# Another sequence of calls on four engines of a fused metaformer layer, with the mixing rows' transposing behind that of t's rows

## What is computed

```
# mixer, on patches of 3x3 positions (j = 0..8), 96 channels
x_norm = sqrt(sum_c patch^2)                  # after a layer norm over channels
y      = patches . w_mask / (x_norm * w_norm) # 512 prototypes, 9 positions
best   = argmax over (prototype, position)
max_act = the patch's channels at the best position     # gathered row of x
vc_vec  = w_mask[best prototype]                        # gathered row
inp  = concat(max_act*max_sim + vc_vec*(1-max_sim), sims of that prototype)
h    = leaky_relu(inp @ w_i1.T + b);  vcs = tanh(h @ w_i2.T + b)
h2   = relu(vcs @ w_l1.T + b) @ w_l2.T + b;  x = x + conv1x1(h2)
# feed-forward, each position a row of 96, weights and inputs rounded to 8 bits
t = x + ffn2(relu(ffn1(layernorm(x))))
```

## Time and profile before

| | before |
|---|---|
| median of 3 runs | 1993.93 us (1993.76 to 1994.25) |
| the profiled execution's own time | 1996.22 us |
| its span, first to last instruction | 1994.4 us |
| PE busy | 1898.1 us, 95% |
| DVE busy | 1866.6 us, 94% |
| ACT busy | 1656.4 us, 83% |
| POOL busy | 1621.8 us, 81% |
| mean granted TensorE clock | 0.985 of full speed |

### The profile page before, as it was taken

One profiled execution on the slowest core, in us unless ns is written; L12 is line 12 of the kernel. 1 busy time (PEld: TensorE's weight loads), 2 busy tenths in 40 slices (PEclk: granted clock), 3 DMA queues, 4 the chain that ended last, 5 costly groups with the idle time before them and its releaser, 6 DMA issues.

```text
span 1994.4 us, 44820 instructions
## 1 busy us (share of the span) xinstructions
PE 1898.1 (95%) x13105; PEld 1429.9 (72%) x13105; DVE 1866.6 (94%) x6525; ACT 1656.4 (83%) x3205; POOL 1621.8 (81%) x1170
## 2 busy tenths in 40 slices
PE   5899999999999999999999999999999999999964
PEld 3567777777777777777777777777777777777642
DVE  7999999999999999999999999999999999999740
ACT  1168888888888888888888888888888888888885
POOL 2578888888888888888888888888888888888752
PEclk9999999999999999999999999999999999999985
DMA  3324545454454545445454454544545455454322
GB/s 96 100 73 129 135 125 147 117 147 125 134 139 117 150 122 139 133 127 145 116 147 126 129 143 117 146 126 133 139 119 151 118 143 129 122 150 118 92 74 71
DMA packets 83890, 249.78 MB, mean 125 GB/s; under 512 B 15736, under 2 KB 17986, under 8 KB 83650
## 3 DMA queue, kind: packets, MB, share of 16 engines
q1 hardware_dynamic: 52866, 170.80, 27.3%
q0 software_dynamic: 28672, 75.52, 18.0%
q10 hardware_dynamic: 2112, 0.60, 0.2%
HBM read 133.23 MB, written 57.02 MB: 95 GB/s over the span
## 4 chain that ended last, share of the span: by engine, by line
PE 72%; DVE 10%; issue 6%; ACT 5%; POOL 3%; DMA 2%; POOLq 0%; SPq 0%; ACTq 0%; DVEq 0%
PE y_ps L648 11%; PE y_ps L650 11%; PE y_ps L649 11%; PE bank L673 9%; PE bank L703 8%; PE bank L685 6%; PE bank L739 4%; ACT y L475 4%; PE bank L754 3%; PE bank L713 3%; DVE best_y L1025 3%; PE bank L723 2%; POOL prod L390 2%; DMA wsel<-proto_rows,w_index 1%; PE bank L711 1%
## 5 line engine op out<-in xcount | busy, mean ns | idle before, releaser
L475 ACT CAST y<-bank 128x384 f16<-128x384 f32 x1152 | 554.1, 481 | 185.9 <-PE bank L673 175.4
L1025 DVE TENSOR_REDUCE best_y<-y_ps 128x2 f32<-128x1024 f32 (+1 forms) x640 | 704.6, 1102 | 0.6 <-PE y_ps L650 0.6
L648 PE MATMUL y_ps<-proto_hi,xh 96*128 96x512 f32 x1152 | 574.1, 498 | 22.5 <-DVE best_y L1025 15.1
L483 ACT ACTIVATE h<-y,f_b 128x1152 f16<-128x1152 f16 x384 | 471.7, 1270 | 0.0
L649 PE MATMUL y_ps<-proto_lo,xh 96*128 96x512 f32 x1152 | 456.5, 396 | 0.0
L650 PE MATMUL y_ps<-proto_hi,xl 96*128 96x512 f32 x1152 | 455.9, 396 | 0.0
L673 PE MATMUL bank<-tqt,f_w 96*128 96x384 f16 x1152 | 390.2, 339 | 42.4 <-ACT y L475 34.7
L411 POOL TENSOR_TENSOR xl<-xc,xh 96x1152 fp32r<-96x1152 f32 x128 | 341.2, 2666 | 26.4 <-ACT xh L538 15.5
L343 POOL DMA_INDIRECT xsel<-x_pm,x_index x128 | 121.6, 950 | 230.0 <-DVE xn L983 216.4
L673 PEld LDWEIGHTS bank<-tqt,f_w 96*128 96x128 f16 x1152 | 110.9, 96 | 262.9 <-issue 144.4
L648 PEld LDWEIGHTS y_ps<-proto_hi,xh 96*128 96x128 f32 x1152 | 221.7, 192 | 84.1 <-issue 39.7
(11 more groups left out here) (131 smaller groups left out, 3874.7 us busy)
## 6 DMA issues: line engine op xcount, KB each, us to landing
xc<-x_cm SPq DMA_DIRECT2D x128, 432.0 KB
xp<-x_pm SPq DMA_DIRECT2D x128, 432.0 KB, 5.4
h<-h POOLq DMA_DIRECT2D x128, 432.0 KB, 4.5
out<-o_pm SPq DMA_DIRECT2D x128, 432.0 KB
xsel<-x_pm,x_index POOLq DMA_INDIRECT x128, 3.7
wsel<-proto_rows,w_index POOLq DMA_INDIRECT x128
proto_rows<-proto SPq DMA_DIRECT2D x1, 384.0 KB, 2.7
proto<-w_mask SPq DMA_DIRECT2D x1, 192.0 KB, 3.3
```

Source lines behind the costliest of these rows:

```text
L475: act.copy(y16[:, q, r * TOK:(r + 1) * TOK], bank[0][:, 0:TOK]).then_inc(s_y16, 1)
L483: act.activation(h16[:, q, :], y16[:, q, :], ACT.Relu, bias=f1_b[:, q:q + 1]).then_inc(s_h16, 1)
L648: pe.matmul(y, hi, proto_hi[:], start=True, stop=False)
L1025: dve.tensor_reduce(best_y[t % 2][:, j0:j1], y_ps[n % 2][:, 0:j1 - j0, :], AX_X, ALU.max).then_inc(s_yd, 1)
```

## The change

No instruction is added or removed, and none gets other operands. Within `slot(s)` the calls stand in another sequence on ACT, PE, POOL and DVE. The core of the diff:

```diff
--- before.py
+++ after.py
@@ -432,14 +432,14 @@
                         in_offset=bass.IndirectOffsetOnAxis(ap=w_index[t % 2][:, 0:1], axis=0)).then_inc(s_wg[t % 2], 16)
 
             def slot(s):
-                gather_x(s)
                 hidden8(s)
                 lock(s)
                 t_norm(s)
+                low_x(s)
+                product(s)
                 t_center(s)
-                product(s)
-                low_x(s)
                 output(s)
+                gather_x(s)
                 low_h(s)
                 gather_w(s)
 
@@ -565,29 +565,29 @@
...
             def slot(s):
+                ffn1_out(s, 0)
                 hidden16(s, FFN2, 2)
-                ffn1_out(s, 0)
+                ffn1_out(s, 1)
+                high(s)
                 vcs_out(s)
-                ffn1_out(s, 1)
                 ffn1_out(s, 2)
+                ffn1_out(s, 3)
+                layer1_out(s)
                 xnt_out(s)
-                high(s)
-                ffn1_out(s, 3)
-                mix_out(s)
-                layer1_out(s)
-                weighted(s)
                 ffn1_out(s, 4)
                 turned(s, 0)
+                weighted(s)
+                mix_out(s)
                 ffn1_out(s, 5)
...
@@ -759,33 +759,33 @@
                 match(s, 0)
                 match(s, 1)
                 ffn1(s, 0)
+                match(s, 2)
+                conv(s, 0)
+                ffn1(s, 1)
                 hidden2(s)
-                conv(s, 0)
-                match(s, 2)
-                ffn1(s, 1)
-                turn_x(s)
-                match(s, 3)
                 ffn1(s, 2)
                 conv(s, 1)
+                match(s, 3)
                 ffn1(s, 3)
-                turn_mix(s)
                 layer1(s)
+                turn_x(s)
+                ffn1(s, 4)
                 match(s, 4)
-                match(s, 5)
-                ffn1(s, 4)
                 turn(s, 0)
                 turn(s, 1)
+                turn_mix(s)
+                match(s, 5)
                 ffn1(s, 5)
...
@@ -1076,43 +1076,43 @@
...
             def slot(s):
+                x_dif(s)
+                low_part(s)
+                cos(s)
                 t_squares(s)
-                low_part(s)
-                mix_sims(s)
...
                 index(s)
-                normed_x(s)
+                mix_sims(s)
+                mix_row(s)
                 root(s, 2)
-                pick_mean(s)
+                pick_root(s)
                 root(s, 3)
                 root(s, 4)
+                root(s, 5)
+                normed_x(s)
+                root(s, 6)
                 residual(s, 0)
-                root(s, 5)
-                pick_root(s)
-                ffn2_bias(s)
-                root(s, 6)
                 y_max(s, 0)
                 residual(s, 1)
                 t_mean(s)
-                remainder(s)
                 y_max(s, 1)
...
```

More of the change, by code:

```diff
@@ L567, in slot @@
             def slot(s):
+                ffn1_out(s, 0)
                 hidden16(s, FFN2, 2)
-                ffn1_out(s, 0)
+                ffn1_out(s, 1)
+                high(s)
                 vcs_out(s)
-                ffn1_out(s, 1)
                 ffn1_out(s, 2)
+                ffn1_out(s, 3)
+                layer1_out(s)
                 xnt_out(s)
-                high(s)
-                ffn1_out(s, 3)
-                mix_out(s)
-                layer1_out(s)
-                weighted(s)
                 ffn1_out(s, 4)
                 turned(s, 0)
+                weighted(s)
+                mix_out(s)
                 ffn1_out(s, 5)
                 turned(s, 1)
+                ffn1_out(s, 6)
+                hidden16(s, FFN, 0)
                 hidden1_out(s)
-                ffn1_out(s, 6)
+                ffn1_out(s, 7)
                 squares(s)
-                ffn1_out(s, 7)
-                hidden16(s, FFN, 0)
                 ffn2_out(s, 0)
+                ffn2_out(s, 1)
                 ffn1_out(s, 8)
-                ffn2_out(s, 1)
                 hidden16(s, FFN, 1)
@@ L761, in slot @@
                 ffn1(s, 0)
+                match(s, 2)
+                conv(s, 0)
+                ffn1(s, 1)
                 hidden2(s)
-                conv(s, 0)
-                match(s, 2)
-                ffn1(s, 1)
-                turn_x(s)
-                match(s, 3)
                 ffn1(s, 2)
                 conv(s, 1)
+                match(s, 3)
                 ffn1(s, 3)
-                turn_mix(s)
                 layer1(s)
+                turn_x(s)
+                ffn1(s, 4)
                 match(s, 4)
-                match(s, 5)
-                ffn1(s, 4)
                 turn(s, 0)
                 turn(s, 1)
+                turn_mix(s)
+                match(s, 5)
                 ffn1(s, 5)
+                pick(s)
+                ffn1(s, 6)
                 match(s, 6)
+                match(s, 7)
                 hidden1(s)
-                ffn1(s, 6)
-                pick(s)
-                match(s, 7)
                 ffn1(s, 7)
@@ L786, in slot @@
                 ffn2(s, 0)
+                ffn2(s, 1)
                 ffn1(s, 8)
-                ffn2(s, 1)
             run.slots(slot)
@@ L1078, in slot @@
             def slot(s):
+                x_dif(s)
+                low_part(s)
+                cos(s)
                 t_squares(s)
-                low_part(s)
-                mix_sims(s)
-                x_dif(s)
+                remainder(s)
+                x_sq(s)
                 x_sum(s)
-                x_sq(s)
-                cos(s)
                 x_norm(s)
-                mix_row(s)
+                best_j(s)
+                ffn2_bias(s)
                 variances(s)
-                best_j(s)
+                one_hot(s)
                 root(s, 0)
-                one_hot(s)
+                pick_mean(s)
                 root(s, 1)
                 index(s)
-                normed_x(s)
+                mix_sims(s)
+                mix_row(s)
                 root(s, 2)
-                pick_mean(s)
+                pick_root(s)
                 root(s, 3)
                 root(s, 4)
+                root(s, 5)
+                normed_x(s)
+                root(s, 6)
                 residual(s, 0)
-                root(s, 5)
-                pick_root(s)
-                ffn2_bias(s)
-                root(s, 6)
                 y_max(s, 0)
@@ L1111, in slot @@
                 y_max(s, 2)
+                best_v(s)
                 x_stats(s, [5])
@@ L1114, in slot @@
                 sims(s)
-                best_v(s)
                 y_max(s, 3)
```

## The result

Both kernels on one chip, medians of four runs each: 2119.43 us after (2113.02 to 2125.81) against 1994.09 before (1993.76 to 1998.36), a ratio of 1.062 [1.059, 1.066]. The change makes the kernel 6% slower, 125 us. The profiled execution of the changed kernel took 2125.81 us.

The account below looks back on a forecast made before the run. PE bounds the kernel before at 14.58 us a slot; the change closes a loop of 10.26 + 5.65 = 15.9 us, and 118 turns of 1.33 us add 157 us, giving 2150 us, range 2070 to 2230.

Parts of the forecast that it names:

- the loop: From `gather_x`'s landing over `xn`, root, lock and five POOL instructions back to `gather_x`: 15.9 us a slot instead of 14.58.
- POOL's 9.61: On POOL, `t_norm`, `t_center`, `product`, `low_x` and `output`, start to start, together 9.61 us of the loop.
- L: Time from `gather_x`'s start to its landing: 5.0 us in a good slot, 5.65 on the mean; binding above 4.2.
- the first rival: The fetch doesn't queue behind `out` and `xc`, lands in about 3 us, PE's 14.5 binds: 1982 us; chance 0.09.
- The share of late slots: For `gather_x`'s landing: four slots in ten late by 1.6 us, raising L from 5.0 to 5.65 on the mean.
- rival 3: The forecast's loop with hardly a late slot: L = 5.0, 15.3 us a slot, +82, 2075 us; chance 0.15.
- 10.26: The loop's sum without L, in us: 0.24 behind `xn`, 0.19 for `ra`, 0.22 to POOL, 9.61 on POOL.
- How PE comes to wait: The late root holds `residual` and `y_max(s, 0)`, so PE's `match` waits for `best_y`, over 1 us a slot.
- The wait ahead of `ffn1`: PE's wait at the `ffn1` behind the transposes for ACT to empty bank 0, about 0.2 us a slot, would go.
- POOL's wait: POOL's idle time moves from `gather_x` to `t_norm`, released by line 1017, about 3 us a slot.
- DVE's order at nothing: The reordered small DVE steps cost nothing, covered by 0.25 us idle a slot; otherwise a tenth of a us a slot.
- PE's 14.5: PE alone would need about 14.5 us a slot after the change, a tenth less than now.

Follow-up runs that it names:

- Experiment 4: The changed kernel with SP issuing the next slot's two loads (`xc`, `xp`) ahead of this slot's store: 1987.19 us, ratio 0.996 to the kernel before.
- Experiment 2: The kernel before with only `gather_x` moved behind `output` on POOL: 2383.99 us, ratio 1.194 to the kernel before.
- experiment 1: The changed kernel with `gather_x` moved back to the head of POOL's slot, ahead of `hidden8`: 2107.34 us, ratio 1.056 to the kernel before.
- experiment 5: The changed kernel with `gather_x` one step further ahead, between `t_center` and `output`: 2128.49 us, ratio 1.066 to the kernel before.
- experiment 7: The kernel of experiment 6 with `best_j` and `index` moved up on DVE, directly behind `cos`: 2041.5 us, ratio 1.023 to the kernel before.
- experiment 6: The kernel of experiment 1 with `product` moved ahead of `low_x` on POOL: 2086.16 us, ratio 1.045 to the kernel before.
- experiment 3: The changed kernel with `normed_x` moved behind `root(s, 6)` on DVE: 2108.13 us, ratio 1.057 to the kernel before.

## Why the prediction was right, and where it was off

**The verdict and the mechanism.** 2119 lies in the range and the loop is as forecast, link by link: POOL's 9.61, the `xn` and root steps, the landing. Experiment 4 shows that L closes it, and that 2.2 of its 5.2 us are a queue behind SP's loads: a change of SP's order alone opened it. Experiment 2 shows that the fetch's place is enough by itself to close the loop. The reading that POOL waited for `index` before, where the earlier trace rows name `xn`, holds as well: `index` starts 1.00 us ahead of the fetch in experiment 1, where the profile names it, and 0.99 before.

**L in a good slot: right, in part by luck.** Forecast 5.0, behind `out` and `xc` and ahead of `xp`. Measured median 5.2, with `xc` landing in 4.4 and `xp` in 5.5. The place in the queue was right. In the changed kernel, from 1019.2 us, where the store is issued, to 1022.4, packets of SP's queue moved and none of POOL's, though the fetch's issue had ended at 1020.42:

```profile
q1 hardware_dynamic: 212, 0.76, 77.2%
```

The parts are off and make up for one another. Counted from the store, the fetch's first packet starts at 3.5 us (median), where the forecast had 4.1; its sixteen packets start over 0.9 us, where it had 0.2; and it lands 1.0 us behind the start of the last, where it had 0.7. The rule of the Trainium skill by which engines take turns between queues, given to the first rival, isn't what these runs show: the first packet starts 3.4 us behind the fetch's start here, and 1.7 in experiment 5, with nothing of SP's ahead of it. With the 1.3 MB beside it the fetch takes 1.7 times as long as with the store alone (3.0), and twice as long as where it lands before the store is issued (2.6).

**The share of late slots: the mis-sized term.** I took four slots in ten at +1.6, L = 5.65 on the mean. A fetch later than 5.6 us is rare here, 4 of 89, and the mean is 5.19, which is rival 3's few late slots: the changed kernel's slots lie between 15.40 and 15.89 us in eight of ten cases. I read the spread from `xp`, the last of the burst; the fetch stands ahead of it and has less of the spread, 4.8 to 5.4 us in eight of ten cases.

**Between `output` and the fetch: a term left out.** 0.16 us a slot of issue. With both put right the loop is 10.26 + 0.16 + 5.2 = 15.6, and 118 x 1.04 = 123 us, against the 125 measured. L on the mean was 0.45 too long, 53 us, and this term 0.16 too short, 19; together 34, against the 31 us by which 2150 was high. With L = 5.2 and without this term the sum gives 2097, at the forecast's lower end: the two errors had opposite signs.

**How PE comes to wait: wrong.** I had the third group of `match` wait for `y_max(s, 0)`, over 1 us a slot. PE waits at `layer1` (line 723) for `t_pm`, 56.4 us in 1400, 0.63 a slot: `residual(s, 0)` is late with the root, and `layer1` needs it sooner. The wait for `best_y` is 0.15 us a slot. Nothing in the sum hung on this. The wait ahead of `ffn1` did go, as forecast: PE's idle time there was 8.7 us in 1400 before and is 0.1 in the changed kernel. But it was worth 0.09 us a slot, where 0.2 was read.

**POOL's wait: half right.** About 3 us at `t_norm` was forecast. It is 1.46 us there and 0.93 at `hidden8`, which waits for ACT: the late slot reaches POOL by ACT as well.

**DVE's order at nothing: right for the changed kernel, wrong as a rule.** DVE was busy for 1375.1 of 1400 us before and 1296.9 after; by the slots of 14.58 and 15.68 us that is 14.3 and 14.5 us a slot, twice the tenth that I had put as the dear case, and hidden by the loop. One instruction makes up the 0.2: `m_sq` (line 940, a product of `m_dif` with itself) now stands beside `low_h` on POOL and is held until that ends. By tile, before and in the changed kernel:

```profile
L940 DVE SCALAR_TENSOR_TENSOR m_sq<-m_dif x95: 169/170/172, 312.8 to 1686.0; 128x9 f32<-128x9 f32 x95
L940 DVE SCALAR_TENSOR_TENSOR m_sq<-m_dif x89: 147/393/416, 314.1 to 1693.6; 128x9 f32<-128x9 f32 x89
```

And the order has a dearer side that the changed kernel doesn't come to pay: `index` late, which makes POOL wait as soon as the fetch leads (moving it up gave 45 us in experiment 7), and `x_dif` first, which is held as soon as `output` runs a little later (in experiment 4 it starts 0.05 us after `output` ends, in the median). The expectation of experiment 1, 1980 to 1992 us with the fetch at the head, failed on that. A prediction from one loop holds for the kernel that has it, and says nothing of what bounds the kernel once it is open.

**PE's 14.5: right.** Where no loop binds and no DVE instruction is held for long (experiment 4, where `m_sq` alone is, by 0.22 us, and the PE and ACT sequences on the kernel before) the slot is 14.50 to 14.53 us. DVE is busy for nearly as long there, 14.4 to 14.5 us a slot, so these runs don't tell the two bounds apart.

## What to carry to other kernels

When an order moves a transfer's issue, follow its result until the chain comes back to that issue; if it does within one turn, no turn can be shorter than the sum of the chain, and the shares of busy time don't show it. Ask of such a transfer what is issued beside it: here a change in who stands ahead of it was worth 132 us (experiment 4), where moving it back on its own engine was worth 12 (experiment 1). And after a loop is opened, look for the next: undoing one part of an order does not give back the old one, because the other engines' sequences were made for each other.

## What the runs showed of the hardware

**A DVE instruction is held while POOL runs one, and the profile calls it busy.** The cases: `m_dif` under `output`, 0.16 to 1.30 us (experiment 5); `m_dif` under `low_h`, 0.43 and 0.45 (experiments 1 and 7); `m_sq` under `low_h`, 0.17 to 0.39 (the changed kernel); `cos` under `low_h`, 0.15 to 0.41 (experiment 6); `xn` under `t_norm`, 0.33 to 1.58 (experiment 3). Each ends 0.02 to 0.07 us after POOL's does. In the kernel before, between 300 and 1700 us, none of these stands beside a computing instruction of POOL's, and none is held. Reductions, of `t_sq` in SBUF or `y_ps`, ran beside the same POOL instructions at their usual time, and so did `t_pm`, of which one input is in PSUM (0.65 us beside `t_norm`).

The Trainium skill has it on the page "SBUF — State Buffer", "Who interferes with whom": a DVE instruction with two SBUF inputs contends with a GpSimd instruction that reads SBUF, and so does `tensor_scalar` in a mode that uses two ports. Which instructions are held agrees in all these cases. The same section says that whoever issues first has the ports for its whole instruction, and the other is blocked. That agrees too: `m_dif` always starts behind `output`, and in experiment 3 an `xn` whose record starts 0.12 us or more ahead of `t_norm`'s is not held (0.32 to 0.39 us), while of the 40 held, 34 start with or behind `t_norm` and 6 up to 0.10 us ahead. The sign to look for is a small DVE instruction whose maximum is far above its minimum with no idle time ahead of it.

The fetch's issue on POOL seems to hold DVE as well, which was not tried by itself: in experiment 3 `cos` starts 0.33 to 0.55 us into it in 30 slots, takes 0.42 to 0.51 us instead of 0.15, and in most of them ends 0.84 us behind the issue's start.

**The time of the fetch's landing follows what was issued ahead of it.** 2.5 us alone, 2.6 where it starts 2.9 us ahead of the store (experiment 5), 3.0 behind the store alone (experiment 4), 5.2 behind the store and `xc` (the changed kernel).
